# Two small product groups of a block plan, and a reciprocal root, take other places in their engines' order

## The reference, cut to what matters

```python
x = x + _L0_attn_ref(_layernorm(x), Wq, Wk, Wv, Wo, rel_bias)      # 8 x 512 x 128
x = x + _L0_ffn_ref(_layernorm(x), keys, w1, b1, w2, b2, rw, rb)
# in the second: logits = -|x - keys|^2 + x @ rw.T + rb
topv, topi = jax.lax.top_k(logits, 4);  w = softmax(topv)
fused = sum over the four of w * (gelu(x @ w1.T + b1) @ w2.T + b2)
```

## Time and profile before

| | |
|---|---|
| median of 3 runs | 1046.58 us (1046.31 to 1049.38) |
| the profiled execution | 1048.65 us, its span 1046.8 us |
| mean granted clock of TensorE | 0.997 of full speed |
| busy share of the span | PE 99%, DVE 81%, ACT 79%, POOL 65% |
| attention steps | from 14.19 us (first scores) to 761.43 us (start of the last step) |

### The profile page before, as it was taken

How to read it: one execution, slowest core, us unless ns; L and a number is a source line. 1 busy time by engine, 2 the same in 40 slices (tenths; PEclk the granted TensorE clock), 3 DMA queues, 4 the chain that set the end, 5 groups by cost and what they waited for, 6 DMA issues and landing times.

```text
span 1046.8 us, 26990 instructions
## 1 busy us (share of the span) xinstructions
PE 1032.5 (99%) x8352; PEld 836.3 (80%) x8353; DVE 843.6 (81%) x2620; ACT 828.3 (79%) x2041; POOL 685.5 (65%) x902
## 2 busy tenths in 40 slices
PE   8999999999999999999999999999999999999997
PEld 5776777777777777777777777777779999999996
DVE  6887889889988988898898889889857676356587
ACT  6887887888888888788878888788877667777673
POOL 5654445777578567757765775777686777766665
PEclk9999999999999999999999999999999999999999
DMA  7566666777577666767666775678852342322285
GB/s 234 152 202 192 192 196 173 207 202 210 167 199 211 202 184 197 215 175 203 187 199 191 205 218 171 195 234 260 254 170 87 119 127 66 109 72 77 85 278 185
DMA packets 135208, 188.51 MB, mean 180 GB/s; under 512 B 18615, under 2 KB 108480, under 8 KB 135072
## 3 DMA queue, kind: packets, MB, share of 16 engines
q1 hardware_dynamic: 126368, 169.91, 55.6%
q0 software_dynamic: 8704, 16.93, 4.8%
HBM read 100.45 MB, written 87.36 MB: 179 GB/s over the span
## 4 chain that ended last, share of the span: by engine, by line
PE 83%; DVE 5%; POOL 4%; issue 3%; DMA 2%; ACT 2%; POOLq 0%; SPq 0%; DVEq 0%; ACTq 0%
PE bank L1635 15%; PE bank L1818 12%; PE bank L1688 10%; PE bank L1704 10%; PE bank L1649 9%; PE bank L1715 4%; PE bank L1584 4%; PE bank L1586 3%; PE bank L1585 3%; PE bank L1802 3%; PE bank L1804 3%; PE bank L1803 3%; POOL shared L1026 3%; PE bank L1774 1%; DVE shared L1303 1%
## 5 line engine op out<-in xcount | busy, mean ns | idle before, releaser
L1026 POOL TENSOR_SCALAR shared<-shared,rinv 128x512 f32<-128x512 f32 x512 | 349.3, 694 | 230.8 <-DVE rinv L1309 228.4
L1113 ACT ACTIVATE shared<-shared,nmax 128x512 f32<-128x512 f32 x512 | 368.6, 733 | 72.2 <-DVE nmax L1303 71.1
L1303 DVE CUSTOM_DVE_ANT_0 shared<-bank,shared 128x512 f32<-128x512 f32 x512 | 329.7, 682 | 72.8 <-PE bank L1649 31.6
L1076 POOL DMA_INDIRECT y_dram<-yb,home x144 | 157.0, 1091 | 75.7 <-issue 56.2
L1322 DVE STREAM_TRANSPOSE turned<-shared 128x512 f32<-128x512 f32 x248 | 161.0, 687 | 1.9 <-issue 1.9
L412 POOL DMA_INDIRECT xs_dram<-copies,slot x128 | 134.3, 1049 | 40.8 <-issue 28.3
L1119 ACT ACTIVATE pt_e<-bank 128x512 f32<-128x512 f32 x256 | 144.7, 594 | 16.8 <-PE bank L1649 16.0
L1818 PE MATMUL bank<-shared,act_h 128*128 x1152 | 140.7, 275 | 0.3 <-ACT act_h L1170 0.3
L1649 PE MATMUL bank<-idn,shared 128*128 128x128 f32 x1024 | 137.1, 276 | 0.5 <-DVE nmax L1303 0.5
L1818 PEld LDWEIGHTS bank<-shared,act_h 128*128 128x128 f32 x1152 | 134.6, 192 | 1.2 <-issue 1.1
L1649 PEld LDWEIGHTS bank<-idn,shared 128*128 128x128 f32 x1024 | 112.9, 141 | 24.3 <-issue 16.3
(11 more groups left out here) (247 smaller groups left out, 1873.1 us busy)
## 6 DMA issues: line engine op xcount, KB each, us to landing
pt_dram<-turned SPq DMA_DIRECT2D x496, 128.0 KB
pt_d<-pt_dram SPq DMA_DIRECT2D x124, 512.0 KB, 4.2
xb<-xs_dram SPq DMA_DIRECT2D x64, 130.0 KB, 2.1
shared<-in_experts SPq DMA_DIRECT2D x16, 514.0 KB
yk_sb<-y_dram SPq DMA_DIRECT2D x24, 256.0 KB, 5.3
shared<-roll_dram SPq DMA_DIRECT2D x3, 768.0 KB, 8.3
y_dram<-yb,home POOLq DMA_INDIRECT x144, 2.6
xs_dram<-pad_sb SPq DMA_DIRECT2D x17, 130.0 KB, 2.2
```

The lines of the kernel that those rows point to most:

```text
L1026: pool.tensor_scalar(tile, tile, rinv[:, 2 * v + hh:2 * v + hh + 1], 1.0, ALU.mult, ALU.mult)\
L1076: pool.indirect_dma_start(y_dram, bass.IndirectOffsetOnAxis(ap=home[:, j, c:c + 1], axis=0), yb[:, j, c, :], None, bounds_check=last_row, ...
L1113: act.activation(prob[:, v, hh, :], prob[:, v, hh, :], ACT.Exp, bias=nmax[:, n:n + 1], scale=-1.0, accum_out=rsum[:, n:n + 1]).then_inc(ex ...
L1303: dve.tensor_tensor_reduce(prob[:, v, hh, :], score_bank(v, hh)[:], strips[:, 2 * i + hh, v * P:v * P + S], -1.0, BIG, ALU.add, ALU.min, n ...
```

## The change

Three edits of order; no instruction is added or taken away.

1. Plan group 0 at (6, 7) moves from `aside_mid` to `aside`, from between the value products to ahead of the late ones.
2. Plan group 2 moves from (7, 1), `aside_mid`, to (7, 2), `aside`; DVE's stage 4, which reads its result, moves from (7, 1) to (7, 2), ahead of stage 5. Group 1 stays.
3. On POOL the stages of routing that stand at a place (i, v) are issued ahead of the scatters of the same place. Only the root at (2, 1) shares its place with a scatter: for b of 2 to 7.

```diff
-        PLAN_DVE_LATE = {(LAST - 1, NPR - 2): ("caps",), (LAST - 1, NPR - 1): (0,), (LAST, 0): (2,), (LAST, 1): (4,), (LAST, 2): (5,)}
-        PLAN_PE = {(LAST - 1, NPR - 1): 0, (LAST, 0): 1, (LAST, 1): 2}
+        PLAN_DVE_LATE = {(LAST - 1, NPR - 2): ("caps",), (LAST - 1, NPR - 1): (0,), (LAST, 0): (2,), (LAST, 2): (4, 5)}
+        PLAN_PE = {(LAST - 1, NPR - 1): 0, (LAST, 0): 1, (LAST, 2): 2}
...
-                    for n, q in scatters_at(b, i, v):
-                        route_pool(pool, n, q)
                     if exists(b - 1):
                         for stage_no in ROUTE_POOL[b].get((i, v), ()):
                             route_pool(pool, b - 1, stage_no)
+                    for n, q in scatters_at(b, i, v):
+                        route_pool(pool, n, q)
...
             def aside(b, i):
...
+                if PLAN_PE.get((b, i)) in (0, 2):
+                    pe.wait_ge(pt_cp, 4 * (b * NPR + i))
+                    plan_pe(pe, 0, aside_bank, PLAN_PE[b, i])
...
             def aside_mid(b, i):
...
-                if (b, i) in PLAN_PE:
+                if PLAN_PE.get((b, i)) == 1:
                     pe.wait_ge(pt_cp, 4 * (b * NPR + i))
                     plan_pe(pe, 0, aside_bank, PLAN_PE[b, i])
```

## The result

The changed kernel takes 1048.95 us (median of 22 runs, 1046.21 to 1058.69), the kernel before 1046.13 us (22 runs, 1043.10 to 1049.38). The ratio is 1.0033 with an interval of 1.0022 to 1.0045: some 3.5 us slower (2.3 to 4.7). I had put 1048.2 us and +1.6 us. So the sign and the range held, and the likeliest case did not: what came out is the rival in which all six sequences pay, which I had priced at +3.6 us and given 17%. The median itself lies only 0.8 us over the 1048.2, and that is chance: my sum stood on 1046.58 us for the kernel before, and its 22 runs give 1046.13. The change, +3.5 us, is what my sum has to answer for.

A forecast was written before the change was run, and what follows sets the result against it. PE was taken to bound the kernel, with 83% of the chain. Three sequences at 0.66 us for the root, less 0.4 for the groups, gave +1.6 us on 1046.58: 1048.2 us, range 1046.1 to 1050.5.

The forecast's parts named there:

- the likeliest case: Whole kernel: three sequences pay 0.66 us each for the root, groups give back 0.4: +1.6 us (+1.2 to +2.4), 58%.
- the rival in which all six sequences pay: POOL's root: six times 0.66 = 4.0 us, less 0.4 for the groups: +3.6 us, 1050.1, 17%.
- The groups: Plan groups 0 and 2 on PE, moved ahead of late value products: 0.2 us gain each, -0.4 us (-0.3 to -0.5).
- The second switch: Possible further switch cost at the start of PE's late value products, raising a group's gain from 0.15 to 0.25 us.
- the rule of the Trainium skill: PE's tiling: mode changes drain, tile changes do not; if single-column weights are a mode, the groups' gain is 0.1 us smaller.
- DVE's stage 4 a pair later: DVE's stage 4 moved from (7,1) to (7,2): cost nothing, at most 0.2 us if the cover were gone.
- The root's size: POOL at (2,2): the root ahead of the scatter waits for `var_eps`, making later blocks 0.66 us later per paying sequence.
- b = 5: Step (5,3), 12.95 us before: POOL's work taken to be the same as in b = 2 and 7, so +0.66 us.
- one-to-one step: Pair 3: POOL's lateness before v = 0 reaches PE in full but for some hundredths; 0.67 more gave 0.64 us.
- Sequences 3 and 6: Steps (3,3) and (6,3): the scatter's 1.45 us gap falls back to 0.78 and pays for the root's wait: 0, otherwise +0.66 each.
- The rule of the Trainium skill that I had named beside the rival: DVE's `k_lo` in (3,2): one SBUF input at most, no contention with POOL, so the long gap need not go.
- Sequence 4: Step (4,3): PE's 1.25 us wait for the DMA into `pt_d` covers the root's delay: 0, otherwise +0.66 us.

The follow-up runs named there:

- the root alone: Kernel before with only the root put ahead of the scatter on POOL, plan groups left in their old places: ratio 1.0022 (1.0006 to 1.0038).
- The second root: Kernel before with a second square root of the same size on POOL ahead of the root, into a tile nobody reads: ratio 1.0080 (1.0061 to 1.0100).
- the groups alone: Kernel before with plan groups 0 and 2 and DVE's stage 4 moved, the scatter still ahead of the root: ratio 1.0001 (0.9984 to 1.0018).
- 3072: Kernel before with dynamic_dma_scratch_size, the room for descriptors, 3072 instead of 4096: 1043.45 us beside 1050.01 of before, one run each.

## Why the prediction held in part

**The groups: right, a little small, and not split evenly.** I had -0.4 us (-0.3 to -0.5); the steps give -0.5 to -0.53. Behind group 0 the early products came down to the 1.73 us that I had named, and the group's own pieces went from 0.60 to 0.43 us. The chain of after in (6,7), as the earlier trace rows:

```profile
671.84 0.26 PE bank L641 x4
672.10 0.17 PE bank L644 x2
672.27 1.88 PE bank L1688 x16
674.15 1.73 PE bank L1704 x16
```

That is 0.15 + 0.17 = 0.32 of the 0.35 us. The second switch, which I had only taken as likely, was there, and in the group's own pieces, not in the late products. Group 2 gained less, 0.15 to 0.2: behind it the early products fell by the same 0.15 us, but its own pieces stayed at 0.15 + 0.06 us. So I had one size for both groups, 0.2, where they gave 0.35 and 0.15 to 0.2. This split is what the rule of the Trainium skill said that I had set beside my sum ("TensorEngine Tiling (Array Packing)", "Key Properties": a change of mode drains, a change of tile doesn't): group 0, of full width like the projections, loses both switches, group 2 only one. The sum that I worked out by it, 0.3 us, was further from the measured 0.5 than my own. By the rule it is the single-column weights that count as a mode of their own; the 0.15 us of L651 in both places, where L641 went from 0.43 to 0.26, agree, and no run here changed their width to show it. DVE's stage 4 a pair later cost nothing, as put.

**The root's size: right.** 0.66 us a sequence was put from POOL's idle time at (1,2); 0.63 to 0.68 came with the root alone. POOL idle ahead of L382, DVE idle ahead of L1322, PE idle ahead of L358, and no slack up to v = 0 are in the rows of after. For b = 5 the number came out by an offset that I hadn't seen: I took POOL's work there to be the same, but the root waited 0.89 us, and 0.24 us of POOL's idle time went in return. The second root confirms the one-to-one step on its own.

**How many sequences pay: wrong, and here lies the error of +1.6 against +3.4.** Six paid, not three.

- *Sequences 3 and 6.* The step that failed is "I take the gap to fall back to 0.78". It rested on one coincidence: the normal start would have fallen on the start of `k_lo`. The same coincidence stood in both places, so seeing it twice was no second witness. The gap belongs to the 28th and 76th scatter: it stayed at 1.46 us when the scatter was moved away from `k_lo`, and (3,3) and (6,3) paid 0.65 us each where I had put 0. It goes with less room for descriptors. The rule of the Trainium skill that I had named beside the rival ("SBUF — State Buffer", "Who interferes with whom") said that an instruction like `k_lo` doesn't contend with POOL; the runs agree with it, and I ought to have given it more than its share of 17%.
- *Sequence 4.* The step that failed is "A PE that comes 0.66 us later waits 0.66 us less: 0". It counted on the 1.25 us that PE waited for `pt_d` in (4,3). In the profiles with the root alone and the groups alone there is no such wait and the step pays 0.64 us. The wait is not made by the order of the program alone: it stood at (4,3) in two of the three profiles on the first chip (before, and 3072 with 14.30 us), and in none of the eight on the others. In after 0.16 us of it stand at (4,3), and the long one stands elsewhere:

```profile
710.44 1.95 PE L1704 MATMUL bank<-pt_d,v_sb 128*64 128x256 f32 x16 [1.24 <-DMA pt_d<-pt_dram]
```

  That is (7,2). Where such a wait falls changes from profile to profile, in place and number, and one profile can't carry a term that rests on it. What makes a transfer late stays open.

**The sum.** 3.9 us for the root less 0.5 for the groups is +3.4 us; the ratio gives +3.5 (2.3 to 4.7). The two agree, as far as an interval of 1.2 us either way can tell.

**The chances.** "All six pay" was a case with a price worked out to 0.2 us, and with that rule of the Trainium skill for it; only a coincidence spoke against it. It should have stood near even with my own sum. The range was drawn wide enough for this rival too, so that it held says nothing for my count of sequences.

## What to carry to other kernels

Before an instruction is put ahead of others on an in-order engine, compare when its input is ready with when it would start: here the input came 0.66 us too late, and since everything behind it was on the path to PE, the whole wait was paid at each of six places. An unexplained gap is to be carried forward as it is, not argued away by what happens to run beside it; count which instance of its kind it is, in both places where it occurs. And a wait for a DMA that one profile shows once is no cover for a delay.

## What the hardware did that I had not expected

- Of the first 100 scatters two started late, after 1.45 us instead of 0.78, always the same two by count, with 4096 for the room for descriptors, and none with 3072 or 2048. Each cost PE 0.64 us where POOL had no slack.
- The same program took 1046 us on one chip and 1081 us on two others, with attention done at much the same time in all (the last step starts between 756.6 and 763.8 us in the eleven profiles). Windows from about 760 us on to the end, before on the first chip and the groups alone on another:

```profile
760.00:1046.00 286.00, 280.86 (x2422) 270.69 (x2418) 185.13 (x571) 195.85 (x502) 196.38 (x197) 1.00 0.41 125
```
```profile
760.00:1078.00 318.00, 292.64 (x2402) 275.75 (x2398) 184.56 (x567) 195.34 (x497) 189.28 (x195) 0.98 0.36 110
```

  DVE and ACT are busy for as long in both, so the 32 us (34, if each is counted from the start of its last step) are not their work. PE is busy 12 us longer at a mean granted clock of 0.98 in place of 1.00, and waits for the rest. The eight register instructions are not the cause: the kernel with 3072 has them too and took 1043.45 us on the first chip. What is stays open. A ratio taken on one chip says what another would show only for the part of the program that runs alike on both.
